# A two-layer graph network with row gathers: one memset and wait behind each gather, or behind every fifth

## The chip, the cores and the metric

The kernel runs on one core of a Trainium2 chip. The metric is the device time of one execution in microseconds. PE is TensorE, DVE is VectorE, ACT is ScalarE, POOL is GpSimd and SP is SyncE. Each engine works through its own instructions in order and waits on semaphores for the others.

## The reference, cut to what matters

```python
# x: (8, 2048, 256) f32, adj: (8, 2048, 2048) 0/1, symmetric, with the diagonal
def layer0(A, X, W, b):                       # S = 25
    scores = where(A != 0, -arange(N), -inf)
    vals, idx = top_k(scores, 25)             # the first 25 neighbours of each row
    feats = X[idx]                            # gathered rows of 256 floats
    agg = max over the 25 (0 joins in where the degree is at most 25)
    return relu(concat([X, agg]) @ W + b)
def layer1(x, A, W, a_src, a_dst, bias, gamma, beta):
    # 4 heads of 64: attention over the neighbours, softmax, relu, + h, norm per head
    ...
x = layernorm(x + layer0(adj, x, W0, b0))
x = layernorm(x + layer1(x, adj, W1, a_src, a_dst, bias, gamma, beta))
```

## The kernel before

The 8 x 2048 rows are 128 tiles of 128 rows, 16 tiles in a batch and 4 tiles in a "quad". Every engine runs the same sequence of steps, one step for a tile. `quad.on(u, lag)` says whether a stage has work in a step. The stages lie apart in time: the mask of a tile is read 3 tiles ahead, its neighbour list is searched 2 tiles ahead, its rows are gathered and reduced in its own step, its residual, norm and projection come one step later, and the attention of layer 1 runs on the batch before (16 tiles behind). So the first 16 steps have no attention, the next 112 have everything, and then 16 steps of attention alone are left.

**GpSimd** has nothing but the gathers. For each tile it waits for the list of indices (`s_idx`), and then works through 5 chunks of 5 gathers (`CH`, `CR`). A gather (line 495) is an indirect DMA which brings one neighbour row of 256 floats to each of the 128 partitions, 128 KB in all. Chunk c has its own buffer `rows[:, c]`; before a chunk GpSimd waits on `s_rfree` until DVE has read the same buffer for the tile before. Behind each gather stands `pace.then(nc.gpsimd.memset(idle[:], 0.0))` (line 498): a memset of 8 floats a partition into a tile that nobody reads, which raises `s_pace`, and a wait of GpSimd for that count. The class `Chain` does this: `then` issues the instruction with an increment and makes the engine wait for it; `end` clears the semaphore.

**DVE** runs, in each step, the search of a later tile: a chain of 35 short operations (lines 737 to 777) in which each waits for the one before. In the places between these links other work is written by hand: 16 operations `uv` of the attention (line 837, at `UNIT_AT`), the residual of layer 0 (lines 787 to 800), `norm0`, which writes `xh` (line 819, at place 25), the maxima over the gathered chunks (line 856, at places 15, 21 and 27 and the last one behind the chain) and the finishing of a quad. A step ends with `aggregate` (lines 865 to 868), which writes `agg`.

**PE** runs, in each step: the product of layer 0, the mask transposes, half of the attention matmuls (line 1258), the transposes of `xh` (line 1236) and the projection, the packing of the mask words (line 1172), three quarters of the other half, the transposes of `xt` and `agg` (line 1213, which wait for `s_agg`), and the rest. In every other step it also spreads `rq` (line 1196) for the next `uv` operations. A `uv` operation can be at most 4 units ahead of the matmuls that read it (`UVB`).

**SP** issues the plain DMAs: `adj`, `xt`, `xh`, `xr` and the output.

Of the kernel before, what the change touches and what calls it, by code (L numbers as in the profile page):

```python
# [92 lines left out]
def run_quads(eng, step):  # L93

    def quad(q, first, last):
        for u in range(QT):
            step(Quad(eng, q, first, last), u)

    def loop(a, b):
        with eng.Fori(a, b) as q:  # L100
            quad(q, a, b - 1)

    quad(0, 0, 0)
    loop(1, BQ - 1)
    quad(BQ - 1, BQ - 1, BQ - 1)
    quad(BQ, BQ, BQ)
    quad(BQ + 1, BQ + 1, BQ + 1)
    loop(BQ + 2, 2 * BQ)
    with eng.Fori(1, B // 2 - 1) as pair:
        for par in range(2):  # L110
            with eng.Fori(0, BQ) as k:
                quad(pair * (2 * BQ) + (k + par * BQ), (2 + par) * BQ, (B - 4 + par + 1) * BQ - 1)
    loop(QUADS - 2 * BQ, QUADS - BQ)
    loop(QUADS - BQ, QUADS - 1)
    quad(QUADS - 1, QUADS - 1, QUADS - 1)
    quad(QUADS, QUADS, QUADS)
    loop(QUADS + 1, QUADS + BQ - 1)
    quad(QUADS + BQ - 1, QUADS + BQ - 1, QUADS + BQ - 1)
    quad(QUADS + BQ, QUADS + BQ, QUADS + BQ)
    quad(QUADS + BQ + 1, QUADS + BQ + 1, QUADS + BQ + 1)  # L120
# [33 lines left out]
def layers_program(nc, x, adj, w0, b0, w1, a_src, a_dst, bias1, gamma, beta,  # L154
# [11 lines left out]
    with ctx:  # L166
        def sb(name, shape, dt):
            return ctx.enter_context(nc.sbuf_tensor(name, shape, dt))
# [78 lines left out]
        idle = sb("idle", [P, 8], F32)  # L247
# [232 lines left out]
        @block.gpsimd  # L480
        def _(pool):
            def step(quad, u):
                if not quad.on(u, 0):
                    return
                for v in quad.reach(lambda q: QT * q + u + 1):
                    pool.wait_ge(s_idx, v)
                pace = Chain(pool, s_pace)
                for c in range(CH):

                    for v in quad.reach(lambda q: CH * (QT * q + u) + c + 1):  # L490
                        pool.wait_ge(s_rfree, v)  # L491
                        pool.sem_inc(s_go["pool"], 1)
                    for r in range(CR):
                        k = c * CR + r
                        nc.gpsimd.indirect_dma_start(  # L495
                            rows[:, c, r * C:(r + 1) * C], None, x_rows,
                            bass.IndirectOffsetOnAxis(ap=idx[u][:, k:k + 1], axis=0)).then_inc(s_rows[c], 16)
                        pace.then(nc.gpsimd.memset(idle[:], 0.0))  # L498
                pace.end()

            run_quads(pool, step)
# [876 lines left out]
```

## Time and profile before

| | |
|---|---|
| median of 3 runs | 5598.53 us (5595.39 to 5600.58) |
| the profiled execution | 5598.51 us, with a span of 5596.7 us |
| POOL busy | 3855.2 us, 69% of the span, 6404 instructions |
| DVE busy | 3947.8 us, 71% |
| PE busy | 3722.0 us, 67%; mean granted clock 0.738 |
| ACT busy | 2181.3 us, 39% |
| gathers (line 495) | 3200, 3469.2 us, 1084 ns mean |
| memsets (line 498) | 3200, 385.8 us, 121 ns mean |

Busy time of POOL is only the time inside gathers and memsets; the time in which GpSimd waits on a semaphore is idle time. A share of busy time is a mean over the three parts of the run (16 steps, 112 steps, 16 steps), which have different work. In a timeline row the part in brackets is how long the engine was idle before the row, and what ended it.

### The profile page before, as it was taken

What the parts mean: (1) busy time and instruction counts of PE and PEld (TensorE: products, weight loads), DVE (VectorE), ACT (ScalarE), POOL (GpSimd) and SP (SyncE); (2) the same over time, 40 slices, a digit from 0 to 9 for tenths busy, and PEclk for the clock granted to TensorE, in tenths of its full rate; (3) what the DMA queues carried; (4) which work ended last, traced back from release to release, by engine and by line L of the source; (5) the groups of instructions that cost most, each with busy time, mean ns of one, the idle gap of its engine ahead of it and who ended that gap; (6) DMA issues with size and microseconds to landing.
All of it is one profiled execution on the core that took longest, in us unless ns stands there. A gap on an engine that the chain in (4) does not pass through costs nothing.

```text
span 5596.7 us, 60889 instructions
## 1 busy us (share of the span) xinstructions
PE 3722.0 (67%) x12546; PEld 1650.0 (29%) x12546; DVE 3947.8 (71%) x12445; ACT 2181.3 (39%) x4674; POOL 3855.2 (69%) x6404
## 2 busy tenths in 40 slices
PE   2232267667676767777777777677777766777787
PEld 1111133323323333333333233323323332333232
DVE  4444477777777777777777777777777777777666
ACT  3333334334444434444443444444344443433212
POOL 5777777777777777777777777777777777777300
PEclk8555577777777777767777777777777777777888
DMA  3333334434334443443444444344444443443100
GB/s 123 116 114 121 114 123 125 131 124 128 123 120 128 130 128 124 128 126 119 129 125 130 125 127 124 122 127 131 128 123 128 125 133 115 133 124 110 54 23 27
DMA packets 264414, 658.87 MB, mean 118 GB/s; under 512 B 62161, under 2 KB 128978, under 8 KB 247762
## 3 DMA queue, kind: packets, MB, share of 16 engines
q0 software_dynamic: 153600, 419.64, 25.9%
q1 hardware_dynamic: 110546, 236.66, 12.1%
q14 instruction: 222, 1.82, 0.1%
q8 instruction: 46, 0.75, 0.1%
HBM read 605.73 MB, written 50.33 MB: 117 GB/s over the span
## 4 chain that ended last, share of the span: by engine, by line
POOL 59%; issue 22%; PE 9%; DVE 7%; ACT 1%; DMA 1%; POOLq 1%; SPq 0%; DVEq 0%; another core or an unknown queue 0%; ACTq 0%
POOL rows L495 53%; POOL idle L498 6%; PE acc L1258 6%; DVE uv L837 2%; DVE rmax L856 1%; DMA rows<-in_x_dram,idx 1%; PE pB L1226 1%; PE rq L1196 1%; PE acc L1184 1%; DVE top L724 1%; ACT raw L574 0%; PE pA L1213 0%; DVE key_b L726 0%; PE pB L1227 0%; POOLq L491 0%
## 5 line engine op out<-in xcount | busy, mean ns | idle before, releaser
L495 POOL DMA_INDIRECT rows<-in_x_dram,idx x3200 | 3469.2, 1084 | 1380.8 <-POOL idle L498 971.4
L1258 PE MATMUL acc<-uv,hs 128*65 128x512 f32 x4096 | 2195.1, 693 | 79.2 <-ACT raw L574 58.8
L837 DVE SCALAR_TENSOR_TENSOR uv<-rq,qinv,maskT 128x512 f32<-128x512 f32 x2048 | 1502.9, 740 | 614.6 <-PE acc L1258 281.4
L1258 PEld LDWEIGHTS acc<-uv,hs 128*65 128x65 f32 x4096 | 629.0, 161 | 1357.2 <-issue 1316.4
L856 DVE TENSOR_TENSOR rmax<-rmax,rows 128x1280 f32<-128x1280 f32 x384 | 570.7, 1486 | 530.6 <-DMA rows<-in_x_dram,idx 530.3
L1236 PE MATMUL pA<-id,xh 128*128 128x128 f32 x256 | 87.4, 444 | 920.7 <-DVE xh L819 906.9
L648 ACT ACTIVATE x1T<-pA 128x256 f32<-128x256 f32 x128 | 49.1, 383 | 1239.3 <-PE pA L1236 1239.3
L639 ACT ACTIVATE xaT<-pA 128x512 f32<-128x512 f32 x128 | 76.4, 597 | 1049.8 <-PE pA L1213 916.3
L1226 PE MATMUL pB<-w_sb,xaT 128*128 128x256 f32 x1024 | 363.2, 517 | 113.5 <-DVE pad L739 67.7
L498 POOL MEMSET idle<- 128x8 f32 x3200 | 385.8, 121 | 2.6
L1236 PEld LDWEIGHTS pA<-id,xh 128*128 128x128 f32 x256 | 36.7, 202 | 1023.3 <-DVE xh L819 1006.9
L1226 PEld LDWEIGHTS pB<-w_sb,xaT 128*128 128x128 f32 x1024 | 259.9, 262 | 248.5 <-DVE pad L739 101.7
L1242 PE MATMUL pB<-wcat,x1T 128*128 128x264 f32 x512 | 271.1, 684 | 60.6 <-ACT x1T L648 60.6
L541 ACT ACTIVATE stage<-pT 128x1024 bf16<-128x1024 f16 x256 | 267.2, 1044 | 89.2 <-remote 43.1
L1213 PE MATMUL pA<-id,xt 128*128 128x128 f32 x256 | 59.6, 319 | 346.0 <-DVE agg L868 345.9
L545 ACT ACTIVATE maskT<-pT 128x1024 f16 (+1 forms) x256 | 267.9, 1047 | 0.0
L1172 PE MATMUL pB<-pack,stage 128*128 128x8 bf16 x2048 | 72.1, 167 | 283.0 <-ACT hs L671 233.3
L524 ACT ACTIVATE stage<-adj_sb,minus 128x2048 bf16<-128x2048 int32 x128 | 254.8, 1991 | 0.0
L856 DVE TENSOR_TENSOR rmax<-rows 128x1280 f32<-128x1280 f32 x128 | 189.3, 1479 | 89.7 <-DMA rows<-in_x_dram,idx 86.5
L574 ACT ACTIVATE raw<-acc,rden 128x64 f32<-128x64 f32 x512 | 111.6, 329 | 344.0 <-DVE rden L879 199.0
L516 ACT ACTIVATE mask_sb<-adj_sb 128x2048 f16<-128x2048 int32 x128 | 243.4, 1902 | 3.9 <-DMA adj_sb<-in_adj_dram 3.9
L724 DVE MAX8 top<-key_b 128x8 f32<-128x104 f32 (+1 forms) x768 | 206.8, 269 | 8.9
(117 smaller groups left out, 4699.4 us busy)
## 6 DMA issues: line engine op xcount, KB each, us to landing
adj_sb<-in_adj_dram SPq DMA_DIRECT2D x128, 1024.0 KB
rows<-in_x_dram,idx POOLq DMA_INDIRECT x3200
xh_dram<-xh SPq DMA_DIRECT2D x128, 256.0 KB
xr<-xh_dram SPq DMA_DIRECT2D x64, 512.0 KB
xt<-in_x_dram SPq DMA_DIRECT2D x128, 128.0 KB
out_dram<-xr SPq DMA_DIRECT2D x32, 512.0 KB
w_sb<-in_L_gnn_W_dram SPq DMA_DIRECT2D x1, 512.0 KB
wcat<-in_L_gnn_W_dram SPq DMA_DIRECT2D x2, 128.0 KB
```

The costliest lines, as they stand in the source:

```text
L495: nc.gpsimd.indirect_dma_start(rows[:, c, r * C:(r + 1) * C], None, x_rows, bass.IndirectOffsetOnAxis(ap=idx[u][:, k:k + 1], axis=0)).then ...
L498: pace.then(nc.gpsimd.memset(idle[:], 0.0))
L516: nc.scalar.activation(mask_sb[:], adj_sb[:], ACT.Sign, accum_out=degree[:, bass.ds(g, 1)]).then_inc(s_mask, 1)
L524: nc.scalar.activation(stage[:].rearrange("p j i -> p (j i)"), adj_sb[:], ACT.Square, scale=2.0, bias=minus1[:], accum_out=adj_sq[:, bass. ...
L541: nc.scalar.activation(stage[:, hf * HALF:(hf + 1) * HALF, :], src, ACT.Square).then_inc(s_stage, 1)
L545: nc.scalar.activation(maskT[:, bass.ds(qg % RING * JT + hf * HALF, HALF), ug * P:(ug + 1) * P], src, ACT.Square).then_inc(s_ring, 1)
L724: ch.then(nc.vector.max(top[:, k:k + 8], a))
L837: stt = nc.vector.scalar_tensor_tensor(uv[k][:, i, :], rq[i][:], inv, m, ALU.max, ALU.mult)
L856: nc.vector.tensor_tensor(rmax[:], before, rows[:, c, :], ALU.max).then_inc(s_rfree, 2 if c == 1 else 1)
L1226: nc.tensor.matmul(p_lin, xaT[:, c, :], w0_sb[:, c, :], start=(c == 0), stop=False)
L1242: nc.tensor.matmul(p_h, x1T[:, c, :], wcat[:, c, :], start=(c == 0), stop=(c == 1))
L1258: last = nc.tensor.matmul(acc[i][0:HW, :], hs[:, (1 - quad.par) * JT + jt, h, :], uv[k][:, i, :], start=(jt == 0), stop=(jt == JT - 1))
```

## The change

The memset and its wait move out of the inner loop: they stand behind the fifth gather of a chunk and no more behind the other four. There are 640 of them in place of 3200. The gathers, their order, their buffers and their semaphores stay as they are. `pace.end()` clears the count after 5 instead of after 25.

```diff
--- before.py
+++ after.py
@@ -495,7 +495,7 @@
                         nc.gpsimd.indirect_dma_start(
                             rows[:, c, r * C:(r + 1) * C], None, x_rows,
                             bass.IndirectOffsetOnAxis(ap=idx[u][:, k:k + 1], axis=0)).then_inc(s_rows[c], 16)
-                        pace.then(nc.gpsimd.memset(idle[:], 0.0))
+                    pace.then(nc.gpsimd.memset(idle[:], 0.0))
                 pace.end()
 
             run_quads(pool, step)
```

## Rows read from the trace of the kernel before

**Rows 1.** The page: span, busy time by engine, chain that ended last by engine.
```profile
span 5596.7 us, 60889 instructions
PE 3722.0 (67%) x12546; PEld 1650.0 (29%) x12546; DVE 3947.8 (71%) x12445; ACT 2181.3 (39%) x4674; POOL 3855.2 (69%) x6404
POOL 59%; issue 22%; PE 9%; DVE 7%; ACT 1%; DMA 1%; POOLq 1%; SPq 0%; DVEq 0%; another core or an unknown queue 0%; ACTq 0%
```

**Rows 2.** Timeline of POOL: start, length, instruction, idle before; fourth and fifth gather, next chunk.
```profile
2500.24 0.95 POOL L495 DMA_INDIRECT rows<-in_x_dram,idx  x1 [0.27 <-POOL idle L498]
2501.19 0.12 POOL L498 MEMSET idle<- 128x8 f32 x1
2501.58 2.02 POOL L495 DMA_INDIRECT rows<-in_x_dram,idx  x1 [0.27 <-POOL idle L498]
2503.60 0.12 POOL L498 MEMSET idle<- 128x8 f32 x1
2504.60 0.95 POOL L495 DMA_INDIRECT rows<-in_x_dram,idx  x1 [0.88 <-POOL idle L498]
```

**Rows 3.** Timeline of DVE in the same stretch.
```profile
2501.30 1.47 DVE L856 TENSOR_TENSOR rmax<-rows 128x1280 f32<-128x1280 f32 x1
```

**Rows 4.** Windows of the three parts: busy us (instructions), granted clock, DMA share, GB/s.
```profile
core 0: us, PE busy (x) PEld busy (x) DVE busy (x) ACT busy (x) POOL busy (x), PEclk, DMA share, GB/s
46.00:691.00 645.00, 175.64 (x900) 111.79 (x897) 311.93 (x1110) 215.68 (x404) 480.63 (x801) 0.57 0.38 119
691.00:5238.00 4547.00, 3255.26 (x10860) 1429.81 (x10860) 3384.45 (x10703) 1871.67 (x4029) 3373.35 (x5599) 0.75 0.40 125
5238.00:5597.00 359.00, 285.46 (x718) 103.47 (x718) 235.73 (x558) 74.44 (x222) 0.76 (x2) 0.85 0.08 25
```

**Rows 5.** Groups of the first part, 46 to 691 us.
```profile
L495 POOL DMA_INDIRECT rows<-in_x_dram,idx x401 | 432.8, 1079 | 209.3 <-POOL idle L498 135.3 <-DVE idx L777 45.3 <-issue 28.8
```

**Rows 6.** Waits of the first part, DVE: us in total, times, longest.
```profile
DVE rmax L856 <- DMA rows<-in_x_dram,idx: 260.2, 64, 5.5
```

**Rows 7.** Groups of the middle part, 691 to 5238 us.
```profile
L495 POOL DMA_INDIRECT rows<-in_x_dram,idx x2800 | 3037.3, 1085 | 1172.7 <-POOL idle L498 836.1 <-issue 318.9 <-DVE rmax L856 14.4
L837 DVE SCALAR_TENSOR_TENSOR uv<-rq,qinv,maskT 128x512 f32<-128x512 f32 x1792 | 1323.7, 739 | 518.9 <-PE rq L1196 236.5 <-PE acc L1258 217.4 <-issue 62.6
```

**Rows 8.** Waits of the middle part.
```profile
PE pA L1236 <- DVE xh L819: 684.5, 109, 12.9
DVE rmax L856 <- DMA rows<-in_x_dram,idx: 358.4, 179, 5.5
...
PE pA L1213 <- DVE agg L868: 161.8, 54, 12.1
```

**Rows 9.** Timeline of all engines, end of a step in which the gathers are late.
```profile
2068.32 1.49 DVE L856 TENSOR_TENSOR rmax<-rmax,rows 128x1280 f32<-128x1280 f32 x1 [2.60 <-DMA rows<-in_x_dram,idx]
...
2071.49 0.41 DVE L868 TENSOR_SCALAR agg<-agg,lim 128x256 f32<-128x256 f32 x1
...
2071.95 0.44 PE L1213 MATMUL pA<-id,xt 128*128 128x128 f32 x2 [2.57 <-DVE agg L868]
```

**Rows 10.** The same for the step behind it.
```profile
2109.01 7.19 PE L1258 MATMUL acc<-uv,hs 128*65 128x512 f32 x11
2110.51 0.58 DVE L868 TENSOR_SCALAR agg<-agg,lim 128x256 f32<-128x256 f32 x1
...
2116.04 0.38 PE L1213 MATMUL pA<-id,xt 128*128 128x128 f32 x2
```

**Rows 11.** Timeline: a short DVE operation that starts 0.54 us into a gather.
```profile
4074.35 0.95 POOL L495 DMA_INDIRECT rows<-in_x_dram,idx  x1 [0.27 <-issue]
...
4074.89 0.41 DVE L745 TENSOR_SCALAR high<-topi 128x26 int32<-128x26 int32 x1
```

**Rows 12.** Timeline: the same operation 0.46 us into another gather.
```profile
706.60 0.95 POOL L495 DMA_INDIRECT rows<-in_x_dram,idx  x1 [0.27 <-issue]
...
707.06 0.16 DVE L745 TENSOR_SCALAR high<-topi 128x26 int32<-128x26 int32 x1
```

**Rows 13.** One line over the whole run: ns min/median/max, first and last start.
```profile
L745 DVE TENSOR_SCALAR high<-topi x128: 160/169/415, 36.5 to 5132.9; 128x26 int32<-128x26 int32 x128
```

**Rows 14.** The page: DMA queues.
```profile
q0 software_dynamic: 153600, 419.64, 25.9%
q1 hardware_dynamic: 110546, 236.66, 12.1%
```

## The prediction

> **What bounds the kernel now.** I read the page first: no engine is busy for more than 71% of the span, yet the chain that ended last runs for 59% on POOL, and much of its "issue" share is POOL's own waiting [rows 1]. So the question is not how busy POOL is but whether it ever rests. The timeline of POOL says what one gather costs: 0.95 us, then 0.12 us of memset, then 0.27 us until the next gather starts, 1.34 us in all; in front of a new chunk the gap is 0.88 us, 0.61 us more [rows 2]. The memset follows its gather without a gap, so GpSimd is through with the gather when the row ends.
>
> The windows cut the run in three [rows 4]. First part, 46 to 691 us: 16 tiles of gathers, no attention. Middle, 691 to 5238 us: 112 tiles with everything. Tail, 359 us: attention alone, no gathers. A tile takes 645 / 16 = 40.3 us in the first part and 4547 / 112 = 40.6 us in the middle. That is POOL's own pace: 25 x 1.34 = 33.5, chunk gaps 5 x 0.61 = 3.1, and 3.3 us by which gathers are longer than 0.95 (3037.3 - 2800 x 0.951 = 374.5 us, over 112) [rows 7]; together 39.9 us, the rest is the branch at the end of a loop. POOL waits for a free buffer for only 14.4 us of the middle [rows 7]. The same excess stands in the first part, 432.8 - 401 x 0.951 = 51.5 us or 3.2 a tile [rows 5]. POOL is the pace-maker in both parts.
>
> In the first part DVE has much room: it waits 260.2 us for gathers, 16.3 us a tile, so without that wait a tile would take it 24 us [rows 6]. In the middle it has little: it waits 358.4 us for gathers, 3.2 us a tile [rows 8], but 518.9 us for PE in front of `uv` [rows 7]. A second loop, DVE, PE and ACT around the attention, runs right behind POOL there. This is the number that caps the gain.
>
> **The change part by part.** *Removed:* 4 of 5 memsets with their waits, 20 a tile. Each is 0.12 + 0.27 = 0.39 us on POOL's path [rows 2], so 7.8 us a tile. *What is left between two gathers:* no gather follows a gather directly in this trace. The nearest rows are the memset, which starts 0.00 us after its gather, and the gather after a wait, at 0.27 us. Lower bound 0, upper bound 0.27. I take 0.03, near the memset's, as the gather will stand in the same queue with nothing to wait for; for both I keep the end at 0.27.
>
> *What gets worse:* a gather that starts while DVE runs an operation with two inputs in SBUF is held until it ends. In [rows 2] the gather of 2501.58 takes 2.02 us; the maximum of [rows 3] ends at 2502.77, and the gather ends 0.83 us after that. It is this that makes up the 374.5 us. With gathers closer together fewer of these operations find a gap: a maximum of 1.48 us now meets a gather that starts, on average, half a period after it. With 1.34 us the delay is 1.48 - 0.67 = 0.81 us, with 0.98 us it is 0.99 us, and shorter operations of the same kind go from about 0.1 to 0.2 us for each of some six a tile (lines 865 to 867 and those of the search). Estimate from these: 1.2 us a tile back. The Trainium skill ("SBUF — State Buffer", who interferes with whom) says the same of a DVE instruction with two SBUF inputs against a GpSimd instruction that reads SBUF; the trace agrees, with 0.83 us from the end of the one to the end of the other.
>
> POOL's tile then is 40.3 - 7.8 + 20 x 0.03 + 1.2 = 34.3 us.
>
> *First part:* POOL stays the pace-maker, as DVE's own 24 us is below 34.3. 16 x (40.3 - 34.3) = 96 us, of which I take 95 (bounds: with 0 between gathers 105, with 0.27 left only 16 x 20 x 0.12 = 38, less the delays).
>
> *Middle:* POOL would save 6.3 us a tile, 706 us, but only what waits for it can be saved. PE's place in a step shows how much. In [rows 9] DVE waits 2.60 us for the last chunk, `agg` ends at 2071.90, and PE, idle for 2.57 us, starts the transposes at once. In the next step `agg` ends at 2111.09 and PE comes to the transposes at 2115.6, since it is still in its attention matmuls [rows 10]: gathers that come earlier would bring nothing there. PE's waits for `agg` total 161.8 us in the middle [rows 8]; this much of the 358.4 us is on the path of both. The remaining 196.6 us of DVE's waits are followed by a wait for PE, or lie in front of `xh`, for which PE waits 684.5 us [rows 8]; those in front of `xh` do move PE. I count a part of them, 28 us, and have 190 us. Lower bound 161.8, upper 358.4.
>
> *Tail:* no gather in it, 0 us. *Start:* the first 46 us wait for the first index list, 0 us.
>
> *On DVE:* short operations such as line 745 are held by a gather too, if they fall into its second half: started at 0.54 us it took 0.41 and ended with the gather [rows 11], at 0.46 us it took 0.16 [rows 12]. The median over 128 is 169 ns, next to the minimum of 160 [rows 13], so the cost is small now; with the gathers 0.98 apart and not 1.34, and 15 such operations a tile (lines 744 to 777 with one tensor input, 819 and 868), it rises by an estimated 0.02 us each, 0.3 us a tile. Part lies under waits for PE; the 28 us above are taken low for it.
>
> *DMA:* the gathers' queue holds the 16 DMA engines for 25.9% of the span [rows 14], 0.45 us a gather (5596.7 x 0.259 / 3200). At 0.98 us apart they still keep up. What is late next: POOL will wait for free buffers in the middle, up to 40.6 - 1.7 - 34.3 = 4.6 us a tile, and costs nothing there.
>
> Sum: 5596.7 - 95 - 190 = 5312 us of span. The execution was 1.8 us over its span and equals the median, so 5313 us.
>
> **Rivals.** *The gap stays:* if a gather starts 0.27 us after the one before even without a wait, only the memset's 0.12 us goes: 38 us in the first part, and in the middle POOL's tile is 38.2 us plus delays, close to the 40.6 - 1.7 = 38.9 us of the other loop, so some 120 us: 5440 us. For it: every gather in the trace has that gap; against: all of them waited for a semaphore.
>
> *All of DVE's wait comes back:* 358 + 105 us, if PE has an answer sooner because its clock rises (granted 0.75 in the middle, 0.85 in the tail, which is denser [rows 4]). Then 5134 us. Against: `agg` was early in [rows 10] and PE was not ready.
>
> *Nothing changes:* the gather itself may go on behind its row and the memset cover it. Then 5598 us. Against: the memset of the same engine takes only 0.12 us right behind it.
>
> *Slower: GpSimd keeps DVE out.* If a gather held the port for its whole length, and in a stream without gaps, each of 15 short DVE operations a tile would wait half a gather, 0.48 us: 7.1 us a tile, 798 us in the middle, and the time is 5597 - 95 - 190 + 798 = 6110 us. It decides against the change from (95 + 190) / (112 x 15) = 0.17 us for each. For it: [rows 11], and no row shows a stream without gaps. Against: [rows 12], where an operation inside the gather is not held. The same page of the Trainium skill gives this rule: the one that starts first has the shared ports for the whole instruction. By that rule the sum would be the 6110 us; the trace agrees only for the second half of a gather (0.41 us against 0.16 us).
>
> **How the numbers follow.** My forecast, 5313 us, has 0.57; its own range is 5260 to 5370, from the 0 to 0.05 us between gathers and 162 to about 230 us in the middle. The gap that stays 0.14, all of DVE's wait 0.13, nothing 0.06, slower 0.10. A difference of 0.2%, 11 us, is what a measurement of this kernel can tell. Faster: 0.57 + 0.14 + 0.13 = 0.84; same 0.06; slower 0.10. The range from 5170 to 5480 takes in the forecast, the gap that stays and a part of the case of 5134, about 0.8.
>
> **What the profile after would show.** Gathers 0.95 us long, with 0.00 to 0.05 us between them inside a chunk; 640 memsets; some 34 us a tile in the first part, which would end near 595 us; in the middle a tile of about 38.9 us, DVE's wait for gathers near zero, POOL's wait for line 856 up from 14.4 to some hundreds of us; PE's wait for `agg` near zero; the tail at 359 us. The prediction is wrong if line 745 and its like are much longer than 169 ns, if gathers are longer than 0.95 us without a maximum beside them, or if PE's clock leaves 0.75 in the middle.

## The result and the profile after

The kernel after takes 5822.83 us (median of 4 runs, 5816.98 to 5834.84), the kernel before beside it 5596.96 us (4 runs, 5587.47 to 5600.58). The ratio is 1.0409, with a 95% interval of 1.0388 to 1.043: 4.1% slower. The profiled execution took 5834.84 us with a span of 5833.0 us.

That is not all of the result. The same kernel, without a letter changed, was run twice more. On chip 1 it took 5370.43 us, a ratio of 0.9587 (0.9548 to 0.9627); on chip 0 it took 5818.12 us, a ratio of 1.0407 (1.0387 to 1.0427). The kernel before took 5585 to 5609 us on all of them. The change is worth -4% on one chip of this kind and +4% on another. The comparison above carries no chip number; its trace looks like the one of chip 0.

The page after: span, busy time, the chain that ended last by engine.

```profile
span 5833.0 us, 58329 instructions
PE 3618.9 (62%) x12546; PEld 1609.2 (28%) x12546; DVE 3925.0 (67%) x12445; ACT 2187.4 (38%) x4674; POOL 3454.9 (59%) x3844
PE 40%; issue 18%; DVE 15%; another core or an unknown queue 11%; POOL 10%; ACT 5%; DVEq 0%; DMA 0%; ACTq 0%; SPq 0%; POOLq 0%
```

The chain has left POOL, 59% in [rows 1] and 10% here, and has 11% on "another core or an unknown queue", where there was 0%. The program has one core, so this is a release for which the profile finds no sender in time.

The timeline of POOL after, against [rows 2]: gathers that follow each other, and the first of a chunk.

```profile
2281.16 0.95 POOL L495 DMA_INDIRECT rows<-in_x_dram,idx  x1 [0.31 <-issue]
2282.41 0.95 POOL L495 DMA_INDIRECT rows<-in_x_dram,idx  x1 [0.30 <-issue]
2283.36 0.12 POOL L498 MEMSET idle<- 128x8 f32 x1
...
2296.53 0.95 POOL L495 DMA_INDIRECT rows<-in_x_dram,idx  x1 [0.88 <-POOL idle L498]
```

A gather starts 0.30 us after the one before it, though it waits for nothing. So a removed memset and its wait save 0.12 + 0.27 - 0.30 = 0.09 us, and not 0.39 - 0.03.

The windows of the three parts after, against [rows 4]. The 401st gather, where the middle begins, starts at 665.0 us, and the last ends at 5470.9.

```profile
core 0: us, PE busy (x) PEld busy (x) DVE busy (x) ACT busy (x) POOL busy (x), PEclk, DMA share, GB/s
46.00:665.00 619.00, 176.25 (x901) 112.14 (x898) 313.12 (x1109) 217.41 (x404) 449.34 (x480) 0.60 0.40 124
665.00:5471.00 4806.00, 3147.73 (x10860) 1386.81 (x10860) 3360.51 (x10703) 1876.12 (x4029) 3005.31 (x3360) 0.74 0.39 118
5471.00:5833.00 362.00, 289.38 (x718) 105.43 (x718) 235.91 (x558) 74.50 (x222) 0.03 (x1) 0.84 0.08 25
```

The first part has become 26 us shorter (619 against 645), 38.7 us a tile. The middle has become 259 us longer (4806 against 4547), 42.9 us a tile against 40.6, and the tail 3 us longer. PE has the same clock there, 0.74 against 0.75. It is the middle that has to be explained, and its groups and waits name what is new.

Groups of the middle after, 665 to 5471 us, against [rows 7]; a line of waits of the whole run for ACT and for DVE.

```profile
L495 POOL DMA_INDIRECT rows<-in_x_dram,idx x2800 | 2936.3, 1049 | 1801.4 <-issue 739.1 <-DVE rmax L856 717.8 <-POOL idle L498 344.5
L837 DVE SCALAR_TENSOR_TENSOR uv<-rq,qinv,maskT 128x512 f32<-128x512 f32 x1792 | 1326.3, 741 | 963.7 <-remote 447.7 <-PE rq L1196 240.3 <-PE acc L1258 230.3
...
ACT stage L541 <- remote: 480.5, 131, 8.9
DVE uv L837 <- remote: 447.7, 52, 12.8
```

GpSimd now stands 717.8 us in front of a buffer that DVE has not read (14.4 before), so it is no longer alone in setting the pace. DVE's wait in front of `uv` has gone from 518.9 to 963.7 us, and "remote" with 447.7 us is as much as the rise. "Remote" stands for the same releases without a sender. What they are can be read in one step (middle, the second step of a quad): PE's mask transposes, the load that follows, and the two engines that wait for PE.

```profile
2273.82 1.07 PE L1158 MATMUL pT<-id,mask_sb 128*128 128x128 f16 x16
2274.72 7.03 PE L1258 MATMUL acc<-uv,hs 128*65 128x512 f32 x16
2274.91 0.02 SPq L397 DMA_DIRECT2D adj_sb<-in_adj_dram  x1
...
2282.15 1.02 ACT L541 ACTIVATE stage<-pT 128x1024 bf16<-128x1024 f16 x1 [7.83 <-remote]
...
2285.05 1.02 ACT L541 ACTIVATE stage<-pT 128x1024 bf16<-128x1024 f16 x1 [0.95 <-remote]
2285.22 0.75 DVE L837 SCALAR_TENSOR_TENSOR uv<-rq,qinv,maskT 128x512 f32<-128x512 f32 x1 [6.87 <-remote]
```

A count is the increment of a semaphore that an instruction makes when it is done. PE ends the 16 transposes of both halves by 2274.9 and goes on with the attention matmuls. The last transpose of each half raises `s_T`, for which line 541 waits, but ACT starts on the first half at 2282.15, more than 7.2 us after both halves were done. DVE's next `uv` needs a count behind the matmuls of line 1258; PE ends those at 2281.75, and DVE starts at 2285.22. PE has done the work; the count of it reaches the others late. (The ends of matmuls are modelled in a trace. In the traces of chips 1 and 7 below, the same model puts every count of PE within 0.1 us of its instruction's end.) Five of GpSimd's gathers run from 2277.39 to 2283.36, the first of ACT's two waits ends in that run, and the other two end 1.7 and 1.9 us after it. In the trace of the kernel before the same wait exists, but is small (whole run):

```profile
ACT stage L541 <- remote: 43.1, 48, 3.0
```

### The profile page after: what moved, and what is told of

It is laid out like the page before. It is cut to its first block, busy times and chain, and to the rows that moved or that the text cites. A ratio compares the mean times of both kernels' runs of the same rounds, so it can differ in the third digit from the quotient of the medians.

```text
span 5833.0 us, 58329 instructions
## 1 busy us (share of the span) xinstructions
PE 3618.9 (62%) x12546; PEld 1609.2 (28%) x12546; DVE 3925.0 (67%) x12445; ACT 2187.4 (38%) x4674; POOL 3454.9 (59%) x3844
## 4 chain that ended last, share of the span: by engine, by line
PE 40%; issue 18%; DVE 15%; another core or an unknown queue 11%; POOL 10%; ACT 5%; DVEq 0%; DMA 0%; ACTq 0%; SPq 0%; POOLq 0%
PE acc L1258 25%; POOL rows L495 10%; DVE uv L837 5%; PE pB L1242 4%; PE pB L1226 2%; DVE rmax L856 2%; PE rq L1196 2%; PE pA L1244 2%; DVE top L724 2%; PE acc L1184 1%; PE pA L1236 1%; ACT hs L671 1%; DVE key_b L726 1%; ACT raw L574 1%
## 5 line engine op out<-in xcount | busy, mean ns | idle before, releaser
L495 POOL DMA_INDIRECT rows<-in_x_dram,idx x3200 | 3376.1, 1055 | 2015.7 <-issue 844.8
L1258 PE MATMUL acc<-uv,hs 128*65 128x512 f32 x4096 | 2167.2, 686 | 216.9 <-ACT raw L574 165.9
L837 DVE SCALAR_TENSOR_TENSOR uv<-rq,qinv,maskT 128x512 f32<-128x512 f32 x2048 | 1505.6, 741 | 1061.2 <-remote 447.7
L1226 PE MATMUL pB<-w_sb,xaT 128*128 128x256 f32 x1024 | 325.2, 473 | 113.8 <-DVE pad L739 57.2
L1226 PEld LDWEIGHTS pB<-w_sb,xaT 128*128 128x128 f32 x1024 | 232.5, 234 | 233.8 <-issue 114.9
L724 DVE MAX8 top<-key_a 128x8 f32<-128x104 f32 (+1 forms) x768 | 207.1, 270 | 5.3
L726 DVE MATCH_REPLACE8 key_b<-top,key_a 128x104 f32<-128x104 f32 (+1 forms) x768 | 199.0, 259 | 0.0
```

Of the source, the lines that this page charges most:

```text
L495: nc.gpsimd.indirect_dma_start(rows[:, c, r * C:(r + 1) * C], None, x_rows, bass.IndirectOffsetOnAxis(ap=idx[u][:, k:k + 1], axis=0)).then ...
L724: ch.then(nc.vector.max(top[:, k:k + 8], a))
L726: ch.then(nc.vector.match_replace(b, top[:, k:k + 8], a, 0.0))
L837: stt = nc.vector.scalar_tensor_tensor(uv[k][:, i, :], rq[i][:], inv, m, ALU.max, ALU.mult)
L1226: nc.tensor.matmul(p_lin, xaT[:, c, :], w0_sb[:, c, :], start=(c == 0), stop=False)
L1258: last = nc.tensor.matmul(acc[i][0:HW, :], hs[:, (1 - quad.par) * JT + jt, h, :], uv[k][:, i, :], start=(jt == 0), stop=(jt == JT - 1))
```

## The experiments

The theory after the result: TensorE's counts come late, and this has to do with how densely GpSimd works. The rival: what the trace shows late is not what costs, and the order of work around the 1 MB load of `adj` or GpSimd's own pace is. The kernels under one heading ran on one chip, but for the last heading, which has two. In the tables a ratio is to the kernel before on the same chip, with its 95% interval.

### Four versions of the pacing and of the load, chip 7

**e1: the load of the next adjacency rows later.** SP waits until ACT has read the transposed mask as well.

```diff
-                    for v in quad.reach(lambda q: QT * q + u + FRONT):
-                        sp.wait_ge(s_adjread, v)
+                    for v in quad.reach(lambda q: 2 * (QT * q + u + FRONT)):
+                        sp.wait_ge(s_ring, v)
```

> The changed kernel, but SP issues the load of the next adjacency tile only when ACT has copied the transposed mask of this one (s_ring), not already when ACT has read adj_sb (s_adjread). In the changed kernel the odd steps lose 7 us between the mask transposes on PE (recorded end 9.8 to 10.7 us into the step) and ACT's start of line 541 (17.1 us); the 1 MB load runs in that stretch. Theory A (PE's count reaches ACT late because the 1 MB load and the gathers fill the DMA engines just then): the wait before line 541 goes, 480 us of waits, and the time falls to 5300 to 5450 us. Theory B (the gathers alone do it, since nothing stands between them): no change, 5800 to 5840 us. Theory C (it is the phase between the engines, DVE being early): anything between, with the wait somewhere else.

**e2: no memset, no wait.**

```diff
-                pace = Chain(pool, s_pace)
...
-                    pace.then(nc.gpsimd.memset(idle[:], 0.0))
-                pace.end()
```

> All memsets and their waits taken out of GpSimd's stream, so a chunk follows a chunk with only the buffer wait. Theory B: a still longer stream holds PE's counts longer, over 5830 us. Theory A: about as the changed kernel, 5800 to 5850 us. First part: about 0.4 us less a chunk than the changed kernel, 2 us a tile, 30 us in all.

**e3: a memset behind each gather, only the fifth waited for.** One column each, so that no two write the same place.

```diff
-                    pace.then(nc.gpsimd.memset(idle[:], 0.0))
+                        if r < CR - 1:
+                            nc.gpsimd.memset(idle[:, r:r + 1], 0.0)
+                        else:
+                            pace.then(nc.gpsimd.memset(idle[:, r:r + 1], 0.0))
```

> A memset of one column behind each gather as before, but only the one behind the fifth is counted and waited for, so GpSimd has the memsets without the waits. If what helped before was the instruction between two gathers: about 5600 us. If it was the wait (an empty queue before each gather), or the slower pace: about 5820 us. Gathers then start 0.30 us behind the memset or sooner.

**e4: a second chained memset behind the fifth gather.**

```diff
                     pace.then(nc.gpsimd.memset(idle[:], 0.0))
+                    pace.then(nc.gpsimd.memset(idle[:], 0.0))
```

> The changed kernel with two chained memsets behind the fifth gather, 0.39 us more a chunk, so that a chunk takes as long as before (7.3 us) while the five gathers stand as close as after. Theory C or any theory of pace: about 5600 us. Theory B (close gathers within the chunk): stays at 5800 us or above.

| chip 7 (before: 5605.69 us) | us | ratio |
|---|---|---|
| e1 later load | 5338.24 | 0.9526 (0.9491 to 0.9562) |
| e2 no memset | 5103.95 | 0.9108 (0.9082 to 0.9135) |
| e3 memsets not waited for | 5353.0 | 0.9553 (0.9525 to 0.958) |
| e4 two behind the fifth | 5406.73 | 0.9649 (0.9621 to 0.9677) |

All four are much faster than the kernel before, e4 too, which is the kernel after with something added. No change to the load explains that, so the kernel after itself had to be run again. Of the pacing alone: e3 has the four memsets back, and its gathers still start 1.25 us apart, as a memset and 0.19 us fit into the 0.30 us that stands between two gathers anyway. e4 did not make a chunk as long as in the kernel before: its second memset starts 0.06 us after the first one ends, so that from one chunk to the next it takes 7.11 us where 7.3 was meant. The kernel after was never run on chip 7, so these four can be set beside it only across chips.

```profile
2503.69 0.95 POOL L495 DMA_INDIRECT rows<-in_x_dram,idx  x1 [0.19 <-issue]
2504.65 0.11 POOL L499 MEMSET idle<- 128x1 f32 x1
2504.95 0.94 POOL L495 DMA_INDIRECT rows<-in_x_dram,idx  x1 [0.19 <-issue]
```

### The kernel after again, chip 1

**e5: nothing edited.**

> The changed kernel once more, without an edit. In its trace PE's counts reached ACT and DVE up to 8 us after the recorded ends; in the traces of e1 to e4 they came within 0.02 us. If the late counts belong to the changed kernel (its order of events), the time is 5815 to 5835 us again and the waits before line 541 are there again. If they belong to the chip or the moment at which it ran, the time falls to 5310 to 5400 us, beside e1, e3 and e4.

**e6: the kernel before with the later load of e1.**

> The kernel before, with the load of the adjacency tile issued after the transposed mask is copied (the edit of e1). In the trace of the kernel before PE's counts behind the mask transposes were late by 0.7 us at the median, up to 4.6. GpSimd is the pace-maker there, so if only it counts, 5590 to 5610 us; if the late counts cost something on the path, down to 5560 us.

**e7: e2 with the later load of e1.**

> No memset at all (e2) and the late load (e1). e2 took 5104 us with no late counts in its trace, so the load has nothing to mend: 5090 to 5130 us. If the load's place matters by itself (adj_sb comes later for ACT's next mask): 5130 to 5200 us.

**e8: the chained memset behind the third and the fifth gather.**

```diff
-                    pace.then(nc.gpsimd.memset(idle[:], 0.0))
+                        if r in (2, CR - 1):
+                            pace.then(nc.gpsimd.memset(idle[:], 0.0))
```

> The chained memset behind the third and the fifth gather of a chunk. By the sum of the gaps (0.09 to 0.12 us a memset on GpSimd's path, and 0.6 us where a chunk ends) it stands 10 to 20 us above the changed kernel's layout without late counts: 5350 to 5420 us. If the changed layout has a bad phase of its own and this one has it too: above 5700 us.

| chip 1 (before: 5608.69 us) | us | ratio |
|---|---|---|
| e5 the kernel after | 5370.43 | 0.9587 (0.9548 to 0.9627) |
| e6 before, later load | 5612.15 | 1.000 (0.998 to 1.0019) |
| e7 no memset, later load | 5119.59 | 0.9139 (0.9102 to 0.9177) |
| e8 two of five | 5451.01 | 0.9731 (0.9691 to 0.9772) |

e5 settles that the kernel's text does not decide between 5370 and 5823. The load does not decide it either: e6 is at no change, and e7 is 16 us above e2, which ran on chip 7. e8 came out above the 5350 to 5420 us expected: it is 81 us above e5, 0.13 us for each of 640 more memsets, where the gaps alone make 0.09; what the rest is, no run shows. In none of the traces from chips 7 and 1 is there a single "remote" wait. The windows of e5, against [rows 4]:

```profile
46.00:663.00 617.00, 176.42 (x895) 112.04 (x893) 312.71 (x1107) 215.08 (x404) 447.61 (x480) 0.56 0.40 124
663.00:5008.00 4345.00, 3210.44 (x10860) 1426.03 (x10860) 3366.32 (x10703) 1866.50 (x4029) 3139.61 (x3360) 0.76 0.42 131
5008.00:5370.00 362.00, 289.42 (x718) 105.50 (x718) 235.86 (x558) 74.42 (x222) 0.00 (x0) 0.84 0.08 25
```

And POOL's waits in e5: us in total, times, longest.

```profile
POOL rows L495 <- issue: 820.5, 2590, 1.5
POOL rows L495 <- POOL idle L498: 520.8, 581, 1.1
POOL rows L495 <- DVE idx L777: 60.2, 14, 44.9
POOL rows L495 <- DVE rmax L856: 18.0, 15, 4.2
```

Here the first part is as long as in the slower run (617 us), and the middle is 202 us shorter than before, 38.8 us a tile. GpSimd waits 18.0 us for buffers, so it is still the pace-maker. Its tile adds up: 25 x (0.95 + 0.30) = 31.3; five chunk ends at 0.12 + 0.88 - 0.30 = 0.70, 3.5; and gathers that are longer than 0.95 us, (3139.6 - 560 x 0.12 - 2800 x 0.951) / 112 = 3.7; together 38.5 us.

### The same on a third chip, chip 0

**e9: the kernel after, nothing edited; e10: e1 again; e11: e2 again.**

> The changed kernel a third time, nothing edited. Theory A (TensorE's late semaphore counts belong to the chip or its state at the first measurement, and GpSimd's order of work sets the time where they are prompt): 5340 to 5400 us and counts passed on at once, or 5800 to 5850 us with counts up to 8 us late in the trace; nothing in between, and the two go together. Theory B (the kernel itself falls into one of two orders of work by chance, whatever the counts do): a slow run with prompt counts, or a fast one with late ones.

> The changed kernel with the 1 MB load held until TensorE has read the mask, the same edit as in the first of these runs, to have it beside the changed kernel on one chip. Where the counts are prompt, theory A: within 40 us of the changed kernel beside it (it was 5338 against 5370 on two chips). Where they are late: if the 1 MB load next to held gathers makes them late, 5340 to 5500 while the changed kernel beside it takes 5800; if the load has no part in it, as slow as the changed kernel.

> No memset and no wait on GpSimd at all, measured closer. Theory A (the pace of GpSimd's queue): 5100 to 5110 us, about 0.91 of the kernel before. Where the counts of TensorE are late it would lose as the changed kernel did or more: 5600 to 5850.

**e12: the chained memset behind the 25th gather of a tile alone.**

```diff
-                    pace.then(nc.gpsimd.memset(idle[:], 0.0))
+                    if c == CH - 1:
+                        pace.then(nc.gpsimd.memset(idle[:], 0.0))
```

> The chained memset only behind the 25th gather of a tile, 1 in a tile in place of 5. Theory A, with GpSimd's queue as the only pace: the changed kernel took 5370 us and the one without memsets 5104, so 266 us for 5 memsets a tile, 53 for each of the five; one is left: 5104 + 53 = about 5157 us. Rival: what the memset behind a chunk costs is paid only where the next chunk's buffer is free already, and with fewer of them the wait for the buffer takes over as without any: 5104 to 5120 us.

| chip 0 (before: 5597.83 us) | us | ratio |
|---|---|---|
| e9 the kernel after | 5818.12 | 1.0407 (1.0387 to 1.0427) |
| e10 after, later load | 5783.94 | 1.0344 (1.0325 to 1.0363) |
| e11 no memset | 6616.18 | 1.1832 (1.1807 to 1.1856) |
| e12 one in a tile | 6605.94 | 1.1807 (1.1779 to 1.1836) |

The first result is back, to 5 us. And the kernel that is the best of all on chip 7, 5104 us, is the worst here, 6616 us: the loss grows as GpSimd's pauses go (before 5598, after 5818, none 6616), all on this chip. It was expected at 5600 to 5850 and is far above; the size was missed, the direction was not. e12 says that one pause in 25 gathers is as none, and its expected 5157 us held for prompt counts alone, which chip 0 does not have. e10 is 34 us below e9: the later load takes back 34 of some 220 us and does not cure the late counts. (Where counts are prompt, e1 is 32 us below e5, but on another chip.)

One stretch of e11 shows the mechanism at its largest. Timelines of POOL, PE, ACT and DVE around 2500 us (line numbers are 1 or 3 lower than in the kernel after).

```profile
2503.85 0.95 POOL L494 DMA_INDIRECT rows<-in_x_dram,idx  x1 [0.30 <-issue]
2527.81 0.94 POOL L494 DMA_INDIRECT rows<-in_x_dram,idx  x1 [23.02 <-DVE rmax L853]
...
2493.29 0.38 PE L1210 MATMUL pA<-id,agg 128*128 128x128 f32 x2
2493.51 1.88 PE L1255 MATMUL acc<-uv,hs 128*65 128x512 f32 x4
2495.32 1.98 PE L1193 MATMUL rq<-er,headsel 4*128 x4
...
2508.12 0.60 ACT L636 ACTIVATE xaT<-pA 128x512 f32<-128x512 f32 x1 [20.87 <-remote]
...
2499.56 0.29 DVE L734 SCALAR_TENSOR_TENSOR key_b<-pB,wordkey 128x128 f32<-128x128 f32 x1 [8.13 <-remote]
2508.44 0.75 DVE L834 SCALAR_TENSOR_TENSOR uv<-rq,qinv,maskT 128x512 f32<-128x512 f32 x1 [8.58 <-remote]
```

PE ends the transposes for `xaT` at 2493.7 and the `rq` matmuls at 2497.3. ACT and DVE, which wait for these two counts, both start at 2508.1 to 2508.4. In between lies the end of GpSimd's run of gathers, at 2504.80: it had no buffer left. The counts came 3.3 us after that. GpSimd stops only when it is blocked, here by DVE, which waits for late counts; so the run of gathers ends with a pause in which only the backlog is worked off (23.02 us here).

### Bytes or issuing, the pause, and more of the pacing: chips 7 and 13

**e13, e17: half the bytes in each gather, no memsets.** The rows are 512 bytes, from another view of `x`; DVE fills the buffers with zero once. So the kernel computes other numbers, and only its time is read.

```diff
-                            rows[:, c, r * C:(r + 1) * C], None, x_rows,
+                            rows[:, c, r * C:r * C + C // 2], None, x_halves,
```

> No memsets, and each gather fetches 512 bytes for a row in place of 1 KB, from half rows (the other half of each buffer stays zero, so the neighbours' maximum is of other numbers). Where TensorE's counts are prompt: GpSimd's pace is set by issuing, 0.95 us and a gap of 0.30 us, and stays; so 5100 us as with full rows, or up to 150 us less if the bytes slow the gathers. Where they are late (6616 us with full rows): if the counts wait for the gathers' bytes in flight, most of the loss goes and the time falls to 5100 to 5600 us with the counts prompt or under 2 us late; if they wait for GpSimd's issuing as such, 6500 to 6650 us with counts as late as before (15 us).

> As e13: no memsets, half the bytes in each gather (half rows, other numbers). Counts prompt: 5087 us again. Counts late (6616 us with whole rows there): 5100 to 5600 if the counts wait for bytes in flight, 6500 to 6650 if they wait for GpSimd's issuing as such.

**e14, e18: GpSimd waits at a chunk's end until the rows have landed.**

```diff
-                    pace.then(nc.gpsimd.memset(idle[:], 0.0))
-                pace.end()
+                    for v in quad.reach(lambda q: 16 * CR * (QT * q + u + 1)):
+                        pool.wait_ge(s_rows[c], v)
```

> Behind the fifth gather of a chunk GpSimd waits until the chunk's rows have landed, with no memset. The wait is some 2.6 us (in the kernel before the vector engine began on a chunk 2.60 us after its last gather) in place of 0.88. Where counts are prompt and GpSimd sets the pace: 640 chunks by 1.7 us more than the changed kernel's 5370 = up to 6460 us, less what other waits covered (5900 to 6460). Where they are late: if a pause of the transfers lets them through, none is over 8 us late, because a chunk takes some 6 us, and the time is near that of a chip with prompt counts, 5900 to 6500; if they don't depend on the pause, they are as late as without memsets (15 us) and the time is over 6700.

> As e14: GpSimd waits behind each chunk until its rows have landed. Counts prompt: 6381 us again. Counts late: within 50 us of that, no count over 8 us late, if a pause of the transfers lets them through; over 6700 us if not.

**e15: e8 again. e16: e3 again.**

> The chained memset behind the third and the fifth gather of a chunk. Where counts are prompt: 5451 us again (5430 to 5470). Where they are late: the kernel before (behind all five) 5598, the changed one (behind the fifth) 5818 there; if the waits on GpSimd let the counts through, this lies between or below both, 5500 to 5700 us; if only a wait behind each gather helps, 5800.

> A memset of one column behind each gather, none but the fifth waited for: the same pauses as the changed kernel. Where counts are prompt: 5353 us again. Where they are late: 5780 to 5850 us as the changed kernel, if it is GpSimd's waits that let the counts through; near 5600 as the kernel before, if the memsets as such do it.

| | chip 7 (before: 5604.44 us) | chip 13 (before: 5584.96 us) |
|---|---|---|
| e13, e17 half the bytes | 5086.62, 0.9075 (0.906 to 0.909) | 6735.02, 1.2041 (1.201 to 1.2072) |
| e14, e18 pause until landed | 6381.31, 1.1386 (1.1367 to 1.1405) | 6384.67, 1.1435 (1.1416 to 1.1454) |
| e15 two of five | 5443.59, 0.9699 (0.9678 to 0.9721) | |
| e16 memsets not waited for | 5354.24, 0.9549 (0.9533 to 0.9565) | |

Chip 13 has late counts, as chip 0 has. Half the bytes cure nothing: 6735 us, above the 6500 to 6650 expected; with whole rows it was 6616 on chip 0. On chip 7 they bring 17 us against 5104. So neither the counts nor GpSimd's pace hang on the bytes in flight, as far as halving them tells. The pause takes the loss away: 6384.67 us on the chip with late counts and 6381.31 on the one without, while the kernel after (5370 and 5818), the one without memsets (5104 and 6616) and the one with half the bytes (5087 and 6735) stand 8, 30 and 32% apart between such chips. It is not only that the slower pace hides late counts: the waits themselves are gone. Whether a pause of this length would do as much without waiting for the rows was not tried. ACT's largest group of waits without a sender in e17:

```profile
ACT xaT L637 <- remote: 2091.4, 104, 35.5
```

And in e18 all that is left of such waits on ACT:

```profile
ACT stage L540 <- remote: 6.5, 9, 1.4
```

The price is the pause itself, 1682.7 us of GpSimd's time, by POOL's waits in e18:

```profile
POOL rows L494 <- DMA rows<-in_x_dram,idx: 1682.7, 604, 5.5
```

Over all traces, the "remote" waits of ACT and of DVE, in us in total, and the time. The last two columns come from the semaphore updates that a trace records: how many counts of PE, between the first and the last gather, arrive over 1.5 us after their instruction's end, and of how many.

```
                             chip      ACT      DVE        us    late      of
before                       not given  43.1      2.4   5596.96    98    1606
after                        not given 480.5    700.2   5822.83   560    1639
e9  after                    0         446.1    667.1   5818.12   541    1636
e10 after, later load        0         393.1    600.2   5783.94   524    1636
e11 no memset                0        2000.3   1625.6   6616.18   646    1768
e12 one in a tile            0        1983.0   1683.2   6605.94   653    1765
e17 half the bytes           13       2277.1   1757.2   6735.02   683    1748
e18 pause until landed       13          6.5      1.5   6384.67    70    1625
e1 to e8, e13 to e16         1 and 7       0        0   5087 to 6381    0
```

So e18 still has some late counts, none by more than 4.1 us, and they cost next to nothing. From "after" to e11 their number rises little, but each is later: the median of the late ones goes from 5.1 to 13.9 us.

## Why the prediction was wrong, and where it was right

**What is left between two gathers** was the first step that failed. I took 0.03 us, by the nearest row, the memset that follows its gather at once; it is 0.30 us on every chip. This was the rival "the gap stays", and I had given it 0.14. The 0.27 us in front of a gather is no price of the wait: the gather has it of itself. The first part, where late counts cost little, shows its worth: 26 us (28 in e5) instead of 95 (bound for this case: 38, less the delays).

**The middle, -190 us.** With prompt counts it is -202 us (e5), but not for my reasons. I let GpSimd go to 34.3 us a tile and let the other loop cap the gain at 38.9. GpSimd went to 38.5 and stayed the pace-maker. It saved 20 x 0.09 = 1.8 us a tile, 202 us over 112; only the sum came out near. The cap itself lies lower than I took it: in e2 GpSimd waits for buffers (334.4 us) and a tile of the middle takes (4739 - 579) / 112 = 37.1 us.

```profile
579.00:4739.00 4160.00, 3131.08 (x10852) 1416.85 (x10853) 3356.54 (x10703) 1866.01 (x4028) 2980.58 (x2800) 0.78 0.43 137
...
4739.00:5099.00 360.00, 290.17 (x727) 104.16 (x725) 235.81 (x558) 74.88 (x224) 0.00 (x0) 0.85 0.08 25
```

**Gathers held by two-input operations of DVE** were right as a mechanism, and the size was off. The excess over 0.951 us was 3.3 us a tile before and is 3.7 in e5, a rise of 0.4 where I had 1.2, because the gathers did not move together as far as I thought (1.25 us apart instead of 0.98).

**Short operations of DVE** stayed what they were: line 745 has a median of 171 ns (169 in [rows 13]) and a maximum of 301. The rival "GpSimd keeps DVE out", 6110 us, did not come. The rule of the Trainium skill ("SBUF — State Buffer", who interferes with whom), that whichever of the two issues first has the shared ports for its whole instruction, does not show in the medians. The page states it for DVE operations in a mode that uses both of its ports; whether line 745 runs in such a mode, no run shows.

**The sign** failed at a step that I did not write down, a term put at nothing without a reason: I took each release as reaching its waiter at once. In the kernel after, 560 counts of PE were over 1.5 us late, ACT and DVE stood 1181 us in waits for such counts, and the middle grew by 259 us where I had -190. "Where POOL waits costs nothing" and "what is late next" were asked of buffers and of DVE alone. On chips 0 and 13 GpSimd's pauses have another use, they let TensorE's counts through. [Rows 1] had 0% for an unknown queue, and the kernel before, with a pause behind each gather, hid it well: its 43.1 us of such waits lay beside GpSimd's own pace. But they were in the trace that the prediction was made from, so that trace is of a chip with late counts. The slower rival was about GpSimd getting in another engine's way, but through DVE's port, with 0.10; the one that came was not among them.

What was shown: the kernel after is faster by 4.1% on chip 1 and slower by 4.1% on chip 0, with the same text (e5, e9). In the slow case releases by TensorE arrive late, and in the fast one none does. Lateness and loss grow as GpSimd's gathers lose their pauses (before, after, e11). The loss goes, and nearly all of the lateness, when GpSimd pauses until the rows have landed (e18 beside e14 and e17). Halving the bytes (e17) does not help, and a later 1 MB load (e10) helps little.

The recorded updates show one thing more. In each of the traces with late counts, PE's counts arrive in exactly the order in which PE raised them, over all its semaphores together, with none out of order (1768 in e11), and a backlog arrives 0.06 us apart. In the stretch of e11 above, the count for the search's `key_b` is the oldest and arrives at 2499.54, in the middle of a run of gathers, 13.2 us late; the next six, on three other semaphores, arrive between 2507.92 and 2508.22. So the counts stand in one line, and a count waits behind all older ones whoever needs it. The oldest one can pass while gathers run: of 104 late counts for `key_b` (line 1169), 99 arrive inside a run of gathers. Most of those behind it pass only when the run ends: of 339 late counts behind line 1255's matmuls in e11, 312 arrive in a pause of GpSimd of over 1 us (such pauses are 32% of the time). A rule of "nothing passes until GpSimd stops" is therefore too simple.

What stays open: why two chips do this and two do not (only chip 7 was used at two different times, and the record does not say which core of a chip ran the program), and what PE's counts share with GpSimd's issuing. The other engines are spared for the most part, not wholly: the count that ACT raises behind line 582 in e11 is 4.2 to 8.1 us late in 25 of 31 records, while it is prompt in the kernel after and in e2, and 3 of some 3700 counts of DVE's search in e11 are late. GpSimd's own are never late. A memset behind every gather with a longer wait was not tried on such a chip, nor were e3 and e8, which might keep the time of before there.

The best version depends on the chip: without any memset 5103.95 us on chip 7 (0.9108), but 1.1832 on chip 0. The kernel before, 5585 to 5609 us on all four, is the one that is safe on every chip measured here.

## What to carry to other kernels

A wait that looks like pure cost on one engine can be what gives the others their turn; before it goes, look in the trace not only for what waits on that engine, but for any wait whose releaser had long been done, however small (43 us here). A gap before an instruction that always follows a wait is not yet the price of the wait; unless a row shows the instruction without one, the gap belongs in the forecast as likely as not. And a result of one chip is a result of one chip: where the sign matters, run the same kernel on more than one before explaining it.

## What the hardware showed that was not expected

- A gather (indirect DMA of 128 rows of 1 KB, or of 512 bytes) takes GpSimd 0.95 us and starts no sooner than 0.30 us after the one before; a memset of 0.11 us fits in between at no cost (gather, memset, 0.19 us, gather).
- Two chips ran one program at two different speeds, 5370 and 5818 us, each within 0.4%, while another program ran at 5585 to 5609 us on these and on two more chips.
- On two of the four TensorE's semaphore counts came late. With five gathers in a row there were waits of up to 12.8 us with no sender in time (the kernel after). With 25 in a row such waits lasted up to 34.3 us (e11, ACT, line 636), and the time rose by 18% over the kernel before.
- Late counts of TensorE kept their order over all semaphores, and a backlog of them arrived 0.06 us apart (e11).
